# A third buffer for the reloaded x, and the first two experts' weights asked for ahead of the routing table

## The reference, cut to what matters

```python
# N = 4096 tokens, F = 256 features, adj dense 0/1 (4096 x 4096, sparse ones + diagonal)
h = layernorm(x)
Wh = h @ W;  src = Wh @ a[:F];  dst = Wh @ a[F:]
att = softmax(where(adj > 0, leaky_relu(src + dst.T, 0.2), -9e15), axis=1)
hp = att @ Wh
gi = hp @ w_ih.T + b_ih;  gh = h @ w_hh.T + b_hh          # a GRU cell
r, z = sigmoid(i_r + h_r), sigmoid(i_z + h_z);  n = tanh(i_n + r * h_n)
x = x + (1 - z) * n + z * h
y = layernorm(x)
logits = y @ gate_w + gate_b                               # 16 experts, the best 2 per token
dispatch = the two largest softmax probabilities, normalised to sum 1
x = x + sum over experts e of dispatch[:, e] * (silu(y @ w1[e]) * (y @ w2[e])) @ w3[e]   # hidden 512
```

## Time and profile before

| | us |
|---|---|
| runs shown | 1231.65, 1233.0, 1241.27 |
| median | 1233.0 |
| the profiled execution | 1236.87 |
| its span in the profile | 1235.1 |

### The profile page before, as it was taken

One profiled execution on the slowest core, in us unless ns is written; L12 is line 12 of the kernel. 1 busy time (PEld: TensorE's weight loads), 2 busy tenths in 40 slices (PEclk: granted clock), 3 DMA queues, 4 the chain that ended last, 5 costly groups with the idle time before them and its releaser, 6 DMA issues.

```text
span 1235.1 us, 26037 instructions
## 1 busy us (share of the span) xinstructions
PE 1140.0 (92%) x7573; PEld 1044.7 (85%) x7574; DVE 1021.7 (83%) x2530; ACT 790.2 (64%) x1157; POOL 423.8 (34%) x417
## 2 busy tenths in 40 slices
PE   5969989999999999999999997199999999999995
PEld 4658979989999999999999996078888888888884
DVE  6966879889999989999999976478888888888783
ACT  2576757766777767777777752166666666666662
POOL 3520112122222222222222201246555555565453
PEclk9889989999999999999999998589999999999998
DMA  8242444445343434343545301242534555534430
GB/s 250 33 68 35 78 48 70 73 59 77 66 80 64 83 49 77 67 80 68 77 69 78 66 18 22 83 139 49 133 68 98 122 146 139 136 62 129 95 49 4
DMA packets 64005, 99.00 MB, mean 80 GB/s; under 512 B 11703, under 2 KB 38328, under 8 KB 63906
## 3 DMA queue, kind: packets, MB, share of 16 engines
q0 software_dynamic: 35824, 52.58, 27.4%
q1 hardware_dynamic: 28082, 45.19, 12.7%
HBM read 213.22 MB, written 19.10 MB: 188 GB/s over the span
## 4 chain that ended last, share of the span: by engine, by line
PE 75%; DMA 11%; DVE 7%; issue 3%; ACT 1%; POOL 1%; SPq 1%; POOLq 0%; DVEq 0%; ACTq 0%
PE bank L1125 14%; PE bank L1380 14%; PE bank L1394 9%; PE bank L1226 9%; PE bank L1225 9%; PE bank L1227 9%; PE bank L1251 6%; DMA out<-ysc,cidx 6%; DMA xin<-in_x 4%; PE bank L1256 3%; PE bank L1277 1%; PE bank L1146 1%; PE bank L1155 1%; DVE xnv L762 1%; DVE pc L807 1%
## 5 line engine op out<-in xcount | busy, mean ns | idle before, releaser
L1225 PE MATMUL bank<-V,pc 128*128 128x258 f32 x1024 | 312.3, 305 | 4.7 <-DVE pc L807 4.7
L1226 PE MATMUL bank<-V,pc 128*128 128x258 f32 x1024 | 292.6, 286 | 0.0
L1227 PE MATMUL bank<-V,pc 128*128 128x258 f32 x1024 | 290.2, 283 | 0.0
L1380 PE MATMUL bank<-wup,xT 128*128 128x512 f32 x948 | 240.0, 402 | 0.9 <-DVE xT L1072 0.9
L514 ACT ACTIVATE pc<-bank 128x512 fp32r<-128x512 f32 x256 | 152.0, 594 | 112.3 <-PE bank L1125 108.1
L807 DVE TENSOR_TENSOR pc<-bank,pc 128x512 fp32r<-128x512 f32 x256 | 175.8, 687 | 48.4 <-ACT pc L514 45.6
L1380 PEld LDWEIGHTS bank<-wup,xT 128*128 128x128 f32 x948 | 174.7, 191 | 35.2 <-DVE xT L1072 1.3
L1225 PEld LDWEIGHTS bank<-V,pc 128*128 128x128 f32 x1024 | 195.2, 191 | 5.8 <-DVE pc L807 5.8
L488 POOL DMA_INDIRECT out<-ysc,cidx x79 | 139.0, 1760 | 170.8 <-DMA out<-ysc,cidx 83.1
L1226 PEld LDWEIGHTS bank<-V,pc 128*128 128x128 f32 x1024 | 197.0, 192 | 0.0
L1227 PEld LDWEIGHTS bank<-V,pc 128*128 128x128 f32 x1024 | 197.0, 192 | 0.0
(11 more groups left out here) (166 smaller groups left out, 1651.9 us busy)
## 6 DMA issues: line engine op xcount, KB each, us to landing
wexp<-in_L_ffn_w SPq DMA_DIRECT2D x237, 512.0 KB
adjb<-in_adj POOLq DMA_DIRECT2D x128, 256.0 KB, 4.7
token_rows<-xrow SPq DMA_DIRECT2D x32, 130.0 KB, 5.7
E<-in_x SPq DMA_DIRECT2D x8, 512.0 KB, 9.0
xin<-in_x SPq DMA_DIRECT2D x32, 128.0 KB, 5.4
out<-xin SPq DMA_DIRECT2D x32, 128.0 KB, 4.5
xg<-token_rows,gidx POOLq DMA_INDIRECT x79
out<-ysc,cidx POOLq DMA_INDIRECT x79
```

Source lines behind the costliest of these rows:

```text
L1225: mm(acc[:, 0:VW], hi, V[:, j, 0, :], start=j == 0, stop=False)
L1226: mm(acc[:, 0:VW], hi, V[:, j, 1, :], start=False, stop=False)
L1227: ins = mm(acc[:, 0:VW], lo, V[:, j, 0, :], start=False, stop=j == T - 1)
L1380: ins = mm(acc[:, 0:HID], xT[:, r % WR, a, k * P:(k + 1) * P], wup[:, r % 2, n, b, k * HID:(k + 1) * HID], start=(k, a, b) == terms[0], st ...
```

## The change

1. `xin` has a third buffer for the reloaded x: tile n uses quarter 0, 1 or 3 by n modulo 3 (`x_of`). There are three semaphores for it. SyncE's step i reloads x(i) and not x(i - 1), after the same wait as before; at i = 2 it waits for the mean terms.
2. Every expert has at least one slot, so its buffer is its number modulo 8, and experts 0 and 1 are loaded by fixed DMAs, into buffers 0 and 1, issued by SyncE behind its tile steps and the end of the last attention chunk. NEW in the table is 0 for them. wup lies first in the memory of the expert phase, wexp behind it.
3. ScalarE splits expert 0 before it waits for the table, and slot 1 before it copies slot 0's tokens. VectorE takes expert 0's low parts ahead of the token indices, slot 1's ahead of slot 0's tokens.

```diff
+    KEPT = 2
...
+        x_of = lambda n: xin[:, (0, 1, 3)[n % 3], :]
...
+        wup = sb("wup", [P, 2, 2, 2, KB * HID], F32R, fs)
         wexp = sb("wexp", [P, WB, 3, KB * HID], F32, fs)
         xg = sb("xg", [P, GR, RW], F32, fs)
-        wup = sb("wup", [P, 2, 2, 2, KB * HID], F32R, fs)
...
+        s_w0 = [sem(f"first_weights_loaded{k}") for k in range(KEPT)]
...
+        def matrix(b, n):
+            return wexp[:, b, n, :] if isinstance(b, int) else wexp[:, one(b), n, :].rearrange("p o f -> p (o f)")
...
             def body(i):
-                if live(i, 1):
-                    v = (i - 1) % 2
+                if live(i, 0):
+                    if i == 2:
+                        sp.wait_ge(s_nmr, 1)
                     if i >= 3:
                         sp.wait_ge(s_x1, i - 2)
-                    sp.dma_start(xin[:, v, :], x[(i - 1) * P:i * P, :]).then_inc(s_xr[v], 16)
+                    sp.dma_start(x_of(i), x[i * P:(i + 1) * P, :]).then_inc(s_xr[i % 3], 16)
...
+            sp.wait_ge(s_mm, T * CPT)
+            for k in range(KEPT):
+                for n, wv in enumerate((w1v, w2v, w3v)):
+                    sp.dma_start(wexp[:, k, n, :], wv[k]).then_inc(s_w0[k], 16)
             sp.wait_ge(s_tab, 1)
...
             def remake_xn(n):
                 v = n % 2
-                act.wait_ge(s_xr[v], (n // 2) * 16 + 16)
+                act.wait_ge(s_xr[n % 3], (n // 3) * 16 + 16)
...
-                nc.scalar.activation(xnb[:, v, :], xin[:, v, :], ACT.Identity, scale=rstd[:, n:n + 1],
+                nc.scalar.activation(xnb[:, v, :], x_of(n), ACT.Identity, scale=rstd[:, n:n + 1],
...
                 waits = []
-                if n == 0:
+                if n == 0 and st is not None and st < KEPT:
+                    waits.append((s_w0[st], 48))
+                if n == 0 and st != 0:
                     waits.append((s_w[r], m * 48 + 48))
...
+            for n in range(2):
+                split_hi(0, 0, 0, 0, 0, n)
+            nc.scalar.activation(silu_warm[:, :], iota_e[:, 0:1], ACT.Silu)
             act.wait_ge(s_tab, 1)
-            nc.scalar.activation(silu_warm[:, :], iota_e[:, 0:1], ACT.Silu)
-            for k in range(2):
-                b = table(act, BUF, k)
-                for n in range(2):
-                    split_hi(k, k, 0, k, b, n)
-                if k == 0:
-                    copy_slot_xT(0, 0, 0)
+            b = table(act, BUF, 1)
+            for n in range(2):
+                split_hi(1, 1, 0, 1, b, n)
+            copy_slot_xT(0, 0, 0)
...
-                V_.tensor_tensor(x1, dd, xin[:, u, :], ALU.add).then_inc(s_x1, 1)
+                V_.tensor_tensor(x1, dd, x_of(i - 2), ALU.add).then_inc(s_x1, 1)
...
-            link(V_.tensor_copy(tiles, ti16[:, 1, :]))
+            link(V_.tensor_single_scalar(tiles, ti16[:, 1, :], 1, ALU.max))
...
-            link(V_.tensor_tensor(tstart, tend, tiles, ALU.subtract))
...
-            link(V_.tensor_scalar(first, tiles, 0.0, float(N), ALU.is_equal, ALU.mult))
-            link(V_.tensor_tensor(first, first, tstart, ALU.add))
-            link(V_.tensor_scalar(tmp, first, pcol[:, 0:1], None, ALU.is_le))
-            link(V_.tensor_reduce(offset, tmp, AX.X, ALU.add))
...
-            link(V_.tensor_copy(sci[:, 0:1], offset))
-            link(V_.tensor_single_scalar(sci[:, 1:2], sci[:, 0:1], WB - 1, ALU.bitwise_and))
...
-            link(V_.tensor_scalar(val[:, NEW:NEW + 1], here, 0.0, used, ALU.is_equal, ALU.mult))
+            link(V_.tensor_scalar(late, expert, float(KEPT), used, ALU.is_ge, ALU.mult))
+            link(V_.tensor_scalar(val[:, NEW:NEW + 1], here, 0.0, late, ALU.is_equal, ALU.mult))
+            link(V_.tensor_copy(sci[:, 0:1], val[:, EXPERT:EXPERT + 1]))
+            link(V_.tensor_single_scalar(sci[:, 1:2], sci[:, 0:1], WB - 1, ALU.bitwise_and))
...
+            for n in range(2):
+                split_lo(0, 0, 0, n)
             dve.wait_ge(s_lt, 1)
             V_.tensor_single_scalar(gidx[:, :], accm[:, 0:SLOTS], float(N - 1), ALU.min).then_inc(s_rd, 1)
             V_.tensor_copy(cidx[:, :], accm[:, 0:SLOTS]).then_inc(s_rd, 1)
...
             dve.wait_ge(s_tab, 1)
-            for k in range(2):
-                b = table(dve, BUF, k)
-                for n in range(2):
-                    split_lo(k, k, b, n)
-                if k == 0:
-                    tokens_lo(0, 0, 0)
+            b = table(dve, BUF, 1)
+            for n in range(2):
+                split_lo(1, 1, b, n)
+            tokens_lo(0, 0, 0)
```

More of the change, by code:

```diff
@@ L239, in gnn_moe @@
         s_x1s = sem("x1_stored")
-        s_xr = [sem(f"x_reloaded{u}") for u in range(2)]
+        s_xr = [sem(f"x_reloaded{u}") for u in range(3)]
         s_ln2 = sem("xn2_done")
@@ L699, in split_hi @@
                     wait_apart(act, *waits)
-                act_copy(wup[:, r % 2, n, 0, :], wexp[:, one(b), n, :].rearrange("p o f -> p (o f)")).then_inc(s_whi, 1)
+                act_copy(wup[:, r % 2, n, 0, :], matrix(b, n)).then_inc(s_whi, 1)
+            for n in range(2):
+                split_hi(0, 0, 0, 0, 0, n)
+            nc.scalar.activation(silu_warm[:, :], iota_e[:, 0:1], ACT.Silu)
             act.wait_ge(s_tab, 1)
-            nc.scalar.activation(silu_warm[:, :], iota_e[:, 0:1], ACT.Silu)
-            for k in range(2):
-                b = table(act, BUF, k)
-                for n in range(2):
-                    split_hi(k, k, 0, k, b, n)
-                if k == 0:
-                    copy_slot_xT(0, 0, 0)
+            b = table(act, BUF, 1)
+            for n in range(2):
+                split_hi(1, 1, 0, 1, b, n)
+            copy_slot_xT(0, 0, 0)
             def slot(s, r, m, st):
@@ L1016, in _, with split_lo, tokens_lo @@
             pair_rows(T + 2)
+            SLOT_LINKS = 2
+            def split_lo(s, r, b, n):
+                wait_apart(dve, (s_whi, s * 2 + (n + 1)))
+                V_.tensor_tensor(wup[:, r % 2, n, 1, :], matrix(b, n),
+                                 wup[:, r % 2, n, 0, :].bitcast(F32), ALU.subtract).then_inc(s_wlo, 1)
+            def tokens_lo(s, r, st):
+                dve.wait_ge(s_fxe, s + 1)
+                V_.tensor_tensor(xT[:, r % WR, 1, :], tp[:, 0:F], xT[:, r % WR, 0, :].bitcast(F32), ALU.subtract).then_inc(s_fxl, 1)
             R = lambda k: r16[:, k, :]
-            total, tiles, tend, tstart, le, tmp, first = (R(k) for k in range(7))
+            total, tiles, tend, le, tmp = (R(k) for k in range(5))
             S = lambda k: sc[:, k:k + 1]
-            expert, start, here, offset, used, near = (S(k) for k in range(6))
+            expert, start, here, late, used, near = (S(k) for k in range(6))
             dve.wait_ge(s_rkr, T)
@@ L1059, in _ @@
             V_.tensor_copy(cidx[:, :], accm[:, 0:SLOTS]).then_inc(s_rd, 1)
[L1062 to L1072, removed]
-            dve.wait_ge(s_tab, 1)
-            for k in range(2):
-                b = table(dve, BUF, k)
-                for n in range(2):
-                    split_lo(k, k, b, n)
-                if k == 0:
-                    tokens_lo(0, 0, 0)
+            dve.wait_ge(s_tab, 1)
+            b = table(dve, BUF, 1)
+            for n in range(2):
+                split_lo(1, 1, b, n)
+            tokens_lo(0, 0, 0)
             slot_base = done[0]
```

## The result

The changed kernel took 1218.25 us (median of 4 runs, 1217.03 to 1220.37) against 1234.67 (4 runs, 1231.65 to 1241.27) for the kernel before: a ratio of 0.987 [0.983, 0.991], faster by 1.3%. 1216 was forecast. The profiled execution took 1217.48 us, with a span of 1215.3: 19.8 less than before.

| stretch | before | after | change | forecast |
|---|---|---|---|---|
| start of the span to the first x1 store | 138.05 | 137.88 | -0.2 | 0 |
| 28 intervals of the x1 stores | 590.07 | 571.39 | -18.7 | -18.7 |
| the last three intervals | 46.86 | 43.64 | -3.2 | 0 |
| last x1 store to the last list positions | 6.69 | 6.69 | 0 | 0 |
| last list positions to the first up product | 24.24 | 25.31 | +1.1 | -2.0 |

What follows compares the result with a forecast made beforehand. TensorE, busy 92% of the span, was taken as the bound, so only its stops could yield time. From the profiled 1236.9 us, 18.7 (reload) and 2.0 (hand-over) were subtracted: 1216.2, say 1216, range 1209 to 1224.

Steps and rivals of the forecast that it cites:

- Part 1: Attention stage: third x buffer and reload asked one tile (20.4 us) sooner remove the late-reload stops, gaining 18.7 us.
- The ruler of the earlier trace: Attention stage: SyncE's x1 stores, one per tile; 28 intervals took 590.1 us against 571.4 at 20.41 each.
- both waits of the earlier trace: Attention stage: ScalarE's 48.6 us for the reloaded x and TensorE's 12.4 us for xn2T, both to disappear.
- Term (a): Hand-over: the last pair scatter, now beside the weight burst, takes 1.9 us longer, ends 0 and +5.0.
- Rival 2: Hand-over: the burst delays pair scatter and lists by the full +5.0 us, giving 1223 us; chance 0.10.
- (b): Hand-over: the gather of the lists, starting as the burst ends, gets 3.0 us shorter, ends -4.2 and 0.
- (c): Hand-over: the first token gather, without weights beside it, gets 0.9 us shorter, ends 0 and -0.9.
- part 2: Hand-over to the experts: early weight loads and splits change the time by -2.0 us, ends -5.1 and +5.0.
- The slots keep their pace, 0: Expert slots: pace stays 5.21 us, one disturbance included, and earlier slot 1 splits gain 0.
- rival 3: Expert slots: moved split buffers lengthen VectorE's work beyond its 1.0 us spare, up to 1240 us; chance 0.03.
- At the end nothing is lost: End of the attention stage: the last reload simply goes out a tile earlier, price 0.
- That tokens decide: Hand-over: the first up product waits for the tokens, over 2 us later than the weights; shortening the weights' path gives 0.

Runs made afterwards that it cites:

- f4: Kernel before without the pair scatters of tiles 0 to 29, leaving most lists unwritten, so only its attention stage compares: 1206.35 us, one run.
- e2: Changed kernel with the old reload (two buffers, x(i - 1) asked for in body i), so the hand-over change alone: 1223.35 us, ratio 1.001 to the kernel before.
- e3: Changed kernel with only wup moved back behind wexp and xg in SBUF: 1215.72 us, ratio 0.994 to the kernel before.
- e1: Kernel before with only the third buffer and the earlier reload, hand-over and slots untouched: 1208.9 us, ratio 0.989 to the kernel before.
- e4: Changed kernel with its six weight loads issued earlier, behind the x1 store of tile 30: 1211.5 us, ratio 0.992 to the kernel before.
- f3: Changed kernel unaltered, run again on chip C: 1216.35 us, ratio 0.993 to the kernel before.
- f1: Changed kernel with the edits of e3 and e4 together, on chip C: 1212.48 us, ratio 0.991 to the kernel before.
- f2: The kernel of e1 run again, on chip C: 1212.01 us, ratio 0.990 to the kernel before.
- g1: Changed kernel with only expert 0 loaded ahead of the table (three loads, 1.5 MB, not six): 1219.28 us, ratio 0.996 to the kernel before.

## Why the prediction was right, and where it wasn't

**Part 1 held as written.** The ruler of the earlier trace rows gave 18.7 and 18.7 came; both waits of the earlier trace rows are gone; nothing else became late. The flight of up to 11.6 us disappears in the 20.4 us that the request was advanced, as argued from the earlier trace rows. f4 adds what the profile of before could not say: why the flights were long.

**Term (a), the pair scatter, was mis-sized.** The prediction took +1.9 from the output scatters of the earlier trace rows, reasoning that a few hundred bytes stand behind a burst. It measured +3.9 on chip A (from the earlier trace rows), and +3.1 to +3.8 between kernels of one chip (e2 and e3 against e1 and e4, f3 against f1 and f2). Rival 2, which put it at up to +5.0, was right in kind. The Trainium skill ("DMA: Bandwidth & Descriptors", section on queues, rings and completion order) states that a DMA engine goes round its queues one whole packet of descriptors at a time, and that a completion increment lands only after all earlier writes of its engine, across the queues. The prediction had this rule and gave it a chance of 0.10. The traces agree in direction (10.25 us against 6.23 in e4), but not in the step: the prediction let the increment wait for the weights, and the packet records show 3.5 us of the 3.9 ahead of the scatter's last word.

**Terms (b) and (c) came out near on chip A**: -2.0 for -3.0 and -0.8 for -0.9, from one pair of profiles. Between kernels of one chip (b) is 0.0 (e1 to e2) and -2.2 (f2 to f3), and (c) is +1.0 in both pairs, the wrong way. So the agreement on chip A is in part luck. On chip A part 2 came to +1.1 in place of -2.0: 2.0 of the difference are (a), 1.0 is (b). Against the same hand-over without the burst it costs more: 23.31 in e2 against 19.50 in e1, 21.61 in f3 against 20.08 in f2.

**"The slots keep their pace, 0" failed**, by 2 us. The prediction looked at what changes in the work and asked in rival 3 only whether VectorE would be slower in its split buffers. The engine that felt the new place was TensorE, which has no slack at all in a slot: 2 ns on each of 948 products. e3 and f1 show the cause: with the old order in memory they are back at 402. (In rival 3 the excess of 0.2 us x 79 slots is 16 us, not 17; nothing hangs on it.)

**"At the end nothing is lost" was right for the transfers and silent on the clock.** The price of the tail depends on whether a stop of 2.5 us halves the clock: 3.1 us to the good here, most likely by chance.

**That tokens decide** held on chip A: the first up product came 1.6 us behind the transposed tokens in both kernels. It holds only just: in e1 and f2 the tokens were faster (2.9 us) and the product waited 0.4 to 1.0 us longer, for the weights.

Together: 1216.2 - 0.2 (start) - 3.2 (tail) + 3.1 (hand-over, +1.1 for -2.0) + 1.2 (slots and end) + 0.4 (2.2 us around the span in place of 1.8) = 1217.5, which is the profiled execution. The forecast was right to 2 us because three misses of 1 to 3 us had different signs; only the -18.7 was known. That is luck. Of its own signs of being wrong two came: the list gather over 9 us behind the last pair scatter, and slots over 5.2 us. And the -20.7 was forecast for the profiled execution, which changed by -19.4; from median to median it is -16.4.

## What to carry to other kernels

Where a transfer is late because of small scattered writes around it, a buffer more and a request one tile sooner was worth the whole wait here and cost nothing. Before moving a bulk load into a gap, look for the small transfer that the next stage waits for in that gap: here the load belonged a tile ahead of it, not 2 us ahead of it, and halving it didn't help. And ask first whether the load is what the next stage waits for: here it wasn't, and the kernel without part 2 is as fast as the one with part 2 repaired. And when a buffer changes its place in SBUF, compare the mean of the bound engine's instructions, not only their number.

## What the runs showed of the hardware

- The place of a product's operand in SBUF shows in its time: 402 ns with wup behind wexp and xg (before, e1, e3, f1), 404 ns with wup ahead of them (changed, e4, f3, g1); without the first 48 products 399 and 401 in all eleven profiles. Why was not tried.
- A scatter of 128 single words takes 5.7 to 6.3 us until its consumer can start, and 9.1 to 10.3 beside 1.5 or 3 MB issued from 2 us ahead on. Of the undisturbed time 4.0 to 4.6 us pass behind its last packet, with next to nothing moving (0 GB/s from 784 to 790 us in the kernel before); the burst delays the packets by 3.5 to 3.8 us. Beside a normal load it is the aggressor: without such scatters the reload's median landing is 2.6 in place of 5.5 us.
- After equal stops of 2.5 us TensorE's clock was halved in some executions and kept in others, 1.55 us each time.
- From the first issue to ScalarE's split, which waits for the first 1.5 MB only, took 10.0 us with nothing issued behind them (g1: 759.38 to 769.38) and 10.8 with 1.5 MB more behind them (changed), both beside the pair scatters.
